# Gated cross-attention block: three score products of two heads stacked in 96 contraction rows, the causal mask as a bf16 matmul, projections one section earlier

## The reference, cut to what matters

```python
q = layernorm(x) @ Wq.T + bq          # split into 16 heads of 16
k = ctx @ Wk.T + bk
v = ctx @ Wv.T + bv
scores = where(causal, q @ k.T / 4, -inf)          # per head, 128x128
x = x + tanh(g_xattn) * ((softmax(scores) @ v) @ Wo.T + bo)
# act_quant: rows scaled to 8-bit integers; weight_quant: weights in {-1,0,1} times a scale
hidden = silu(bitlinear(layernorm(x), w_gate)) * bitlinear(layernorm(x), w_up)
x = x + tanh(g_ffn) * bitlinear(hidden, w_down)
```

## Time and profile before

| | us |
|---|---|
| median of 3 runs (1930.03 to 1931.12) | 1930.83 |
| profiled execution | 1932.1 |
| its span, first to last instruction | 1930.4 |
| busy: PE / PEld | 1747.9 (91%) / 1396.7 (72%) |
| busy: DVE / ACT / POOL | 1658.1 (86%) / 1434.1 (74%) / 1053.1 (55%) |
| granted TensorE clock, mean | 0.990 |
| HBM and SBUF traffic by DMA | 91.22 MB, mean 47 GB/s |

### The profile page before, as it was taken

The page is one execution under the profiler, slowest core; times in us unless marked ns, Lnnn a source line. Parts: engine busy times, 40 slices in busy tenths (PEclk is TensorE's granted clock), DMA queues, the critical chain, the costliest instruction groups (busy, mean ns, idle before and its releaser), DMA issues. The chain is left out here.

```text
span 1930.4 us, 46249 instructions
## 1 busy us (share of the span) xinstructions
PE 1747.9 (91%) x15430; PEld 1396.7 (72%) x15430; DVE 1658.1 (86%) x3609; ACT 1434.1 (74%) x2897; POOL 1053.1 (55%) x1623
## 2 busy tenths in 40 slices
PE   3799999999999999999999999999999999999984
PEld 2677777777777777777777777777777777777762
DVE  4588988988988888888898898898898898898884
ACT  3577777787777787777777777777777777778772
POOL 4455555556556556555555555555555555655641
PEclk9999999999999999999999999999999999999996
DMA  3222122122122122122122222222212212212210
GB/s 106 45 53 44 43 53 46 42 55 49 37 56 48 37 57 48 38 55 48 40 52 48 43 50 50 44 47 53 42 46 53 43 45 53 50 38 56 48 20 11
DMA packets 131900, 91.22 MB, mean 47 GB/s; under 512 B 13521, under 2 KB 131409, under 8 KB 131665
## 3 DMA queue, kind: packets, MB, share of 16 engines
q1 hardware_dynamic: 130416, 88.13, 22.4%
q10 hardware_dynamic: 1248, 0.14, 0.1%
HBM read 37.88 MB, written 16.78 MB: 28 GB/s over the span
## 5 line engine op out<-in xcount | busy, mean ns | idle before, releaser
L507 PE MATMUL psum<-k_blk,q_t 128*128 128x512 f32 x1536 | 419.1, 408 | 1.2 <-DVE q_t L935 1.2
L1041 POOL TENSOR_SCALAR xc<-x,ln 128x256 f32<-128x256 f32 x128 | 61.3, 479 | 485.5 <-DVE ln L898 485.5
L849 DVE TENSOR_REDUCE row_max<-psum 128x8 f32<-128x1024 f32 x256 | 311.2, 1215 | 7.1 <-PE psum L507 6.9
L507 PEld LDWEIGHTS psum<-k_blk,q_t 128*128 128x128 f32 x1536 | 268.8, 188 | 62.1 <-issue 14.1
L717 ACT ACTIVATE prob<-psum,row_max 128x128 f32<-128x128 f32 x1024 | 277.4, 385 | 12.7 <-DVE row_max L849 12.6
L1064 POOL TENSOR_SCALAR hq<-h,sm 128x1024 f16<-128x1024 f32 x128 | 143.2, 1119 | 226.6 <-DVE sm L929 220.5
L724 ACT COPY prob_t<-psum 128x1024 f32<-128x1024 f32 x256 | 262.4, 1025 | 5.1 <-PE psum L515 1.4
L515 PE MATMUL psum<-ident,prob 128*128 128x128 f32 x2048 | 255.1, 273 | 4.4 <-ACT prob L711 3.9
L515 PEld LDWEIGHTS psum<-ident,prob 128*128 128x128 f32 x2048 | 228.8, 141 | 6.6 <-ACT prob L711 5.1
L732 ACT ACTIVATE th<-psum,sm 128x512 f32<-128x512 f32 x256 | 178.8, 698 | 14.9 <-PE psum L607 13.2
L872 DVE SCALAR_TENSOR_TENSOR gu<-th,psum 128x512 f32<-128x512 f32 x256 | 174.9, 683 | 10.9 <-ACT th L732 6.8
(11 more groups left out here) (116 smaller groups left out, 3729.9 us busy)
## 6 DMA issues: line engine op xcount, KB each, us to landing
k_blk<-k_t SPq DMA_DIRECT2D x512, 64.0 KB, 2.4
c_in<-in_ctx SPq DMA_DIRECT2D x64, 256.0 KB
x_in<-in_x SPq DMA_DIRECT2D x64, 256.0 KB
out<-y SPq DMA_DIRECT2D x128, 128.0 KB
g_nat<-in_L_ffn_w_gate SPq DMA_DIRECT2D x1, 1024.0 KB, 10.5
g_nat<-in_L_ffn_w_up SPq DMA_DIRECT2D x1, 1024.0 KB, 12.8
g_nat<-in_L_ffn_w_down SPq DMA_DIRECT2D x1, 1024.0 KB, 14.4
w_nat<-in_L_xattn_Wq SPq DMA_DIRECT2D x1, 256.0 KB, 4.1
```

The costliest lines, as they stand in the source:

```text
L507: last = nc.tensor.matmul(dst, q_t[:, b, a, half, c.s, :], k_blk[:, w, half, c.s, 4 * b:4 * b + 4, :], start=n == 0, stop=n == len(TERMS) - 1)
L849: nc.vector.tensor_reduce(out=row_max[:, HPC * half:HPC * (half + 1)], in_=S_B[half].rearrange("p (h k) -> p h k", k=P), axis=AX.X, op=ALU ...
```

## The change

- Scores: `k_blk` and the selectors go. For two heads, the three products stand below each other in 3 x 32 = 96 contraction rows (`q_stk`, `k_stk`), so one matmul of 256 columns gives the scores of two heads. Half a tile takes four of these, behind two bf16 matmuls of 512 columns (identity by `causal`) that put the mask into PSUM.
- DMAs: six per pair for K (128 KB each), three for Q (256 KB each), into two buffers by pair; every contiguous run is 2 KB.
- Softmax: PE transposes the shifted scores (`s_low`), and ACT's exp reads them from PSUM and writes `prob_t`. ACT shifts half 1 with Identity.
- Q is split on POOL (`split_qk`) in place of ACT `q_high` and DVE `q_low`. The bias-added x lies in three buffers, and the copy `keep_residual` goes.
- Projections: context and K in B for the pair after next, x, Q and V in A for the next. The walk begins a pair earlier. Every engine has one order for A and B, which is B's.

```diff
-            for i in range(-1, PAIRS + 2):
-                for c in sections(2 * i):
-                    body(c)
+            for i in range(-2, PAIRS + 2):
+                for s in range(2):
+                    body(Section(i, s))
...
+                self.proj = i + 1 + s
+                self.norm = s == 1 and 0 <= i + 2 < PAIRS
...
                 def spread_k(c):
-                    for g in range(HPC):
-                        rows = slice(HD * g, HD * (g + 1))
-                        sp.dma_start(k_blk[rows, :, :, :, g, :].rearrange("p a c s k -> p (a c s) k").bitcast(F32),
-                                     k_t[rows, :, :, :, :].rearrange("p a c s k -> p (a c s) k").bitcast(F32)).then_inc(kb_ld, 16)
+                    for n, part in enumerate(K_STACK):
+                        for a in range(2):
+                            at = n * PAIR_HD + a * HD
+                            sp.dma_start(k_stk[p % 2][at:at + HD, a].rearrange("e h c s k -> e h (c s k)").bitcast(F32),
+                                         k_t[64 * a:64 * a + 64, part].rearrange("p c s k -> p (c s k)").bitcast(F32)
+                                         ).then_inc(k_ld, 16)
+                def spread_q(c):
+                    for n, part in enumerate(Q_STACK):
+                        sp.dma_start(q_stk[p % 2][n * PAIR_HD:(n + 1) * PAIR_HD].rearrange("e h c s q -> e h (c s q)").bitcast(F32),
+                                     q_t[:, part].rearrange("p c s q -> p (c s q)").bitcast(F32)).then_inc(q_ld, 16)
...
                 def body(c):                       # SP
+                    if c.spread:
+                        spread_k(c) if c.s == 0 else spread_q(c)
+                    load_ctx in B, store, load_x in A
...
-                def scores(c, half):
-                        for n, (a, w) in enumerate(TERMS):
-                            last = nc.tensor.matmul(dst, q_t[:, b, a, half, c.s, :],
-                                                    k_blk[:, w, half, c.s, 4 * b:4 * b + 4, :],
-                                                    start=n == 0, stop=n == len(TERMS) - 1)
+                def scores(t, half):
+                    wait(pe, p_ok[half], t)
+                    for b in range(2):
+                        nc.tensor.matmul(S_B[half][:, b * BANK:(b + 1) * BANK], ident_b[:, :],
+                                         causal[:, :].unsqueeze(1).to_broadcast((P, 4, P)),
+                                         start=True, stop=False, skip_group_check=True)
+                    pe.wait_ge(k_ld, 6 * 16 * (p + 1))
+                    pe.wait_ge(q_ld, 3 * 16 * (p + 1))
+                    for g in range(4):
+                        h, c = (4 * half + g) // DC, g % DC
+                        last = nc.tensor.matmul(S_B[half][:, 2 * g * P:(2 * g + 2) * P], q_stk[p % 2][:, h, c, s, :],
+                                                k_stk[p % 2][:, :, h, c, s, :],
+                                                start=False, stop=g % 2 == 1, skip_group_check=True)
...
+PE, both sections:   quant_t, scores(t, 1), inputs_t, out_natural, hidden_t, out_t, down, gate_up 0, out_proj,
+                     project_qk, shifted_t 0, shifted_t 1, gate_up 1, project_v (A), scores(t + 1, 0), values
+ACT, both sections:  quant_t, inputs_t, hidden_t, out_t, shift, tanh 0, project_qk, exp 0, tanh 1, exp 1,
+                     project_v (A), values
+DVE, both sections:  top 0, shift, out_natural, top 1, norm_stats (B), out_t, result, residual, gated 0,
+                     first_norm (B), row_scales, gated 1, hidden_scales
+POOL, both sections: split_inputs, centre, first_norm (B), add_bias (A), quantise, quantise_hidden, split_qk
...
                 def exp(c, half):
+                    nc.scalar.activation(prob_t[:, HPC * half:HPC * (half + 1), :].rearrange("p h k -> p (h k)"),
+                                         S_B[half], ACT.Exp).then_inc(p_ok[half], 1)
```

More of the change, by code:

```diff
@@ L184, in _ @@
                                          scale=(SCALE, 1.0, 1.0, tgates[:, 0:1])[n]).then_inc(w_hi, 1)
[L189 to L199, removed]
                 for n in range(3):
@@ L416, in tile @@
             def tile(self, back):
-                return self.even + (self.ahead + self.s + 1 - back)
+                return self.t + 1 - back
             def pair(self, back):
[L420 to L437, removed]
+                return 2 * (self.proj + 1 - back)
@@ L476, in store @@
                 def store(c):
-                    wait(sp, y_ok, c.tile(3))
-                    hold(sp)
-                    tile = c.even + (c.s - 3)
-                    sp.dma_start(out[tile], y[:, 1 - c.s, :]).then_inc(y_st[1 - c.s], 32)
+                    sp.wait_ge(y_ok, c.tile(3))
+                    sp.dma_start(out[c.t - 3], y[:, 1 - c.s, :]).then_inc(y_st[1 - c.s], 32)
                 def body(c):
-                    if c.s == 0 and c.more:
+                    if c.spread:
+                        if c.s == 0:
+                            spread_k(c)
+                        else:
+                            spread_q(c)
@@ L484, in body @@
+                    if c.s == 1 and c.more:
                         load_ctx(c)
-                    if c.s == 1 and c.proj:
-                        spread_k(c)
                     if c.down:
                         store(c)
-                    if c.s == 1 and c.more:
+                    if c.s == 0 and c.more:
                         load_x(c)
@@ new lines, in body @@
+                    if c.ffn:
+                        quant_t(c)
+                    if c.attn:
+                        scores(c.t, 1)
+                    if c.projects:
+                        inputs_t(c)
+                    if c.outp:
+                        out_natural(c)
+                    if c.down:
+                        hidden_t(c)
+                    if c.outp:
+                        out_t(c)
+                    if c.down:
+                        down(c)
+                    if c.ffn:
+                        gate_up(c, 0)
@@ new lines, in body @@
+                    if c.outp:
+                        out_proj(c)
+                    if c.projects:
+                        project_qk(c)
+                    if c.attn:
+                        shifted_t(c, 0)
+                        shifted_t(c, 1)
+                    if c.ffn:
+                        gate_up(c, 1)
+                    if c.projects and c.s == 0:
+                        project_v(c)
+                    if c.ahead:
+                        scores(c.t + 1, 0)
+                    if c.attn:
+                        values(c, 0)
+                        values(c, 1)
@@ L705, in _, with shift @@
             def _(act):
-                def exp(c, half):
-                    if half == 0:
-                        act.wait_ge(s_sub, c.tile(0))
-                        v = prob[:, 0:HPC, :]
-                        nc.scalar.activation(v, v, ACT.Exp).then_inc(s_exp[0], 1)
-                        return
+                def shift(c):
                     act.wait_ge(s_max[1], c.tile(0))
@@ new lines, in body @@
+                    if c.ffn:
+                        quant_t(c)
+                    if c.projects:
+                        inputs_t(c)
+                    if c.down:
+                        hidden_t(c)
+                    if c.outp:
+                        out_t(c)
+                    if c.attn:
+                        shift(c)
+                    if c.ffn:
+                        tanh(c, 0)
+                    if c.projects:
+                        project_qk(c)
+                    if c.attn:
+                        exp(c, 0)
@@ L840, in _ @@
+                    if c.ffn:
+                        tanh(c, 1)
+                    if c.attn:
+                        exp(c, 1)
+                    if c.projects and c.s == 0:
+                        project_v(c)
+                    if c.attn:
+                        values(c)
                 walk(act, body)
@@ L847, in top @@
                     dve.wait_ge(s_mm[half], c.tile(0))
-                    wait(dve, s_exp[1] if half == 1 else s_sub, c.tile(1))
+                    wait(dve, s_sub[half], c.tile(1))
                     nc.vector.tensor_reduce(out=row_max[:, HPC * half:HPC * (half + 1)],
@@ new lines, in body @@
+                    if c.attn:
+                        top(c, 0)
+                        shift(c)
+                    if c.outp:
+                        out_natural(c)
+                    if c.attn:
+                        top(c, 1)
+                    if c.norm:
+                        norm_stats(c)
+                    if c.outp:
+                        out_t(c)
+                    if c.down:
+                        result(c)
+                    if c.outp:
+                        residual(c)
@@ L1014, in _ @@
+                    if c.ffn:
+                        gated(c, 0)
+                    if c.norm:
```

(21 more changed lines are left out.)

467 lines of the change are left out of this document (127 added, 340 removed).

## The result

The changed kernel takes 1963.39 us (median of 4 runs, 1961.37 to 1965.01), the kernel before 1930.74 (median of 4, in the same comparison): a ratio of 1.0169, 95% interval 1.0151 to 1.0187. It is slower by 32.7 us, against a forecast of no change (1931) and 1.4 us above the upper end of the forecast range.

What follows compares the result with a forecast made beforehand. It took a chain through DVE, PE and ACT in section B as the bound: B gains 1.1 us, A gives back 1.1. The terms, -4 for 62 pairs and +5 at the start, gave 1931 us, own range 1916 to 1944, eight-in-ten range 1914 to 1962.

Steps and rivals of the forecast that it cites:

- The loop: Chain through DVE, PE and ACT from one section's `top` 0 to the next, put at 14.25 us in the changed kernel.
- What bounds the kernel: In section B one chain that changes engines sets the time, neither PE nor DVE being full; held with 0.62.
- PE's scores beside the loop: Score matmuls are not on the chain, so freeing 1.9 us of PE per pair lies beside it.
- The size of the score saving: Half a tile of scores on PE goes from 1.46 us to 0.99, freeing 0.47 per half.
- the term for the moved statistics: Layer norm statistics on DVE in B, ahead of the `o_t` subtraction, make B 0.15 us longer: 14.40.
- The ends: Start of the walk: first scores wait for POOL's Q split, its DMAs and two more weight DMAs; +5 us, once.
- rival 2: POOL, or another branch with under 0.1 us of slack, becomes late: +12 to +37 us, 1943 to 1968; chance 0.18.
- rival 3: Q's DMAs land later than 12.3 us after `top` 0: up to +37 us, 1968; chance 0.08.
- rival 1: PE's occupation sets the time: a pair falls by 1.9 us, the time to 1818; chance 0.07.
- rival 4: The rest, such as a clock below 1.00 with PE idle 14% of the time: slower; chance 0.05.
- The sum itself: -4 us for 62 steady pairs and +5 for the start make +1, given as 1931 us, range 1916 to 1944.

Runs made afterwards that it cites:

- e2: Changed kernel with each mask matmul issued twice, the second adding to the first; 1962.46 us, ratio 1.0136 to 1.0180 to the kernel before.
- e1b: Changed kernel with DVE's layer norm statistics moved behind the down projection's `result`, run again for its trace; 1926.12 us.
- e3: Changed kernel with a fourth Q DMA of 256 KB per pair into unused rows, which the scores wait for too; 2169.73 us.
- e6: Changed kernel with each mask matmul issued four times in place of once; 2093.15 us.
- e4: e1b's edit on the changed kernel, plus `gate_up` 1 ahead of PE's transposes and ACT and DVE reordered to match, in both sections; 1879.79 us.
- e8: e4 with Q's three DMAs cut into six by tile, and each mask matmul issued twice; 1916.45 us, 47.6 us more than without the doubled masks.

## Why the prediction was wrong

The forecast was no change; the kernel is 32.7 us slower. The loop was right and one link of it was left out.

- What bounds the kernel: right. The loop's starts after `top` 0 in A, worked out and measured: `out_t` 3.15 and 3.15, `down` 3.43 and 3.43, `out_proj` 5.15 and 5.13, `project_qk` 5.93 and 5.92, `gate_up` 1 9.08 and 9.08, `gated` 1 10.88 and 10.86, the section 14.25 and 14.20.
- PE's scores beside the loop: right in sign, and shown by e2. But that 1.7 us per pair cost nothing at all is in part luck: in B `out_proj` waited for `y` anyway, which hid 0.25, and part of the masks fell into the wait for Q (its median fell from 0.88 to 0.42). The room itself was 0.6 of the 0.86 added, not the 0.3 that I gave it.
- The size of the score saving: I put 0.99 for a half tile; one takes 1.03 from its first mask matmul to the next group (931.58 to 932.61). The changed kernel's PE is busy 1.7 us per pair less than before by the two windows (25.13 against 26.86), near the 1.9.
- **The step that failed** is the term for the moved statistics, "B is 0.15 longer". It followed the `o_t` subtraction alone (to 5.29; measured 5.21) and took `out_proj` to wait for that. But `out_proj` also has a wait on `y_ok`, and `result` stands behind the subtraction on DVE. It ended at 5.60 and `out_proj` began at 5.75. So the link is 0.6 longer than in A, four times what I had put down. Over 62 pairs the difference of 0.41 between 28.6 and 29.01 is 25 us. e1b removes the whole link: both sections at 14.2, 1926.12 us.
- The ends: +5 was put down. The start was +6.4, near it. The last section and the tail, which I left out, were another 6.3 in the profiled execution, 2.4 of them with the granted clock of 0.79 in the last section A. In e2, with the same orders and a clock of 1.00 there, the two were 2.4 above the kernel before.
- POOL (rival 2): its branch was never late. The split of x or context ended 5.66 after `top` 0, 0.2 before PE wanted it. In A `project_qk` began at 5.92, in e1b at 5.91 in both sections.
- Q's landing (rival 3): 12.0 us after `top` 0, inside 8.3 to 12.9, but at its slow end; I had leaned to the fast one. One term was missing: SP issued the DMAs at 3.70, their packets ran from 4.9 to 10.5, and the last landing came at 11.9, 1.4 us behind the last packet, for which the sum had nothing. That it stayed in the range is luck in part. The wait cost the changed kernel nothing (e1b), and e3 shows that it was close to costing much.
- PE bound (rival 1): refuted by e2 and e6.
- The clock (rival 4): 1.00 from 88 to 1880 us of the changed kernel's trace, so it had no part in the longer pairs.
- The sum itself: +1 on the kernel before's 1930.83 is 1932 and not 1931, and the terms' bounds (-11 to +2 for the pairs, +4 to +9 for the start) give 1924 to 1942, not 1916 to 1944. Neither slip bears on the miss.

## What to carry to other kernels

When the profile shows one chain that passes through several engines again and again, a saving beside it is worth nothing, however costly its group is on the page. First shorten the chain, as e4 did, and then the saving counts, as e8 shows. For an instruction that is moved within an engine's order, list every semaphore that every later instruction of that engine releases before the next wait, and not only the first; place it where the engine waits anyway, with the length of that wait at hand (1.14 us for 0.74 here). One order for two kinds of section is simpler, but here it gave the fast section the slow one's loop.

## What the runs showed of the hardware that I had not expected

Transfers within SBUF gained little from longer runs. With 512-byte runs K's spread moved 107 GB/s at a share of 0.75, and 100 over its middle 5 us. K's spread with 2 KB runs (and DMAs of 128 KB in place of 64) began at about 210 for a microsecond and then moved 125. First the kernel before, then the changed one:

```profile
1021.00:1026.00 5.00, 5.00 (x42) 4.37 (x40) 3.50 (x11) 4.92 (x12) 2.50 (x5) 1.00 0.76 100
```

```profile
910.00:914.00 4.00, 4.00 (x34) 3.61 (x33) 3.16 (x11) 2.74 (x6) 2.73 (x5) 1.00 1.11 125
```

Q's spread, also with 2 KB runs, starts at 225 GB/s in its first microsecond and falls to the same level:

```profile
922.50:923.50 1.00, 0.63 (x3) 0.10 (x1) 0.90 (x3) 1.00 (x5) 0.95 (x1) 1.00 0.93 225
924.00:925.00 1.00, 1.00 (x11) 1.00 (x10) 0.43 (x1) 0.81 (x2) 0.00 (x0) 1.00 1.13 129
925.00:926.00 1.00, 1.00 (x11) 1.00 (x10) 0.93 (x5) 0.06 (x1) 0.00 (x0) 1.00 1.09 125
```

There the share says that the DMA engines are occupied all the time (it can pass 1, as it adds up packets that overlap), yet they move 125 to 129 GB/s, against 301 for a load at a share of 0.86. The estimate from the Trainium skill's port rule (SBUF — State Buffer, Door 1: The DMA port swizzle), 218 GB/s for 32 partitions, is met in the first microsecond alone. The 109 that the same rule gave for K, near the 107 of the 512-byte runs, is passed by K's 125 to 210 with 2 KB runs. What limits these transfers afterwards is left open.

A PE wait of 2.97 us in e3 was followed by matmuls at 1.19 us for a group of 0.71, while the waits of 0.86 and 1.18 us in the changed kernel left the granted clock at 1.00. In between it is not the wait's length alone: of the waits for Q in e1b, five of 1.54 to 1.84 us were followed by a lower clock, while others of up to 1.82 us were not.
